# Left one-hots of a graph kernel's count matrix, groups innermost, code numbers read from SBUF

## What is computed

```
def step(h, _):
    messages = h[col] @ W_msg.T + b_msg
    agg = segment_sum(messages, row, num_segments=num_nodes)
    gi = agg @ W_ih.T + b_ih
    gh = h @ W_hh.T + b_hh
    r = sigmoid(i_r + h_r);  z = sigmoid(i_z + h_z)
    n = tanh(i_n + r * h_n)
    return ((1.0 - z) * n + z * h, None)
h, _ = lax.scan(step, relu(layernorm(x)), None, length=5)
return x + h
```

## Time and profile before

| | us |
|---|---|
| median of 3 runs | 5297.94 (5295.67 to 5298.79) |
| span of the profiled execution | 5295.2 |
| VectorE's first L1368 to its last L1374 | 219.5 to 834.3 |
| GpSimd's first L674 to its last | 117.2 to 960.9 |
| TensorE's first product on gathered rows | 976.5 |

### The profile page before, as it was taken

How to read it: one execution, slowest core, us unless ns; L and a number is a source line. 1 busy time by engine, 2 the same in 40 slices (tenths; PEclk the granted TensorE clock), 3 DMA queues, 4 the chain that set the end, 5 groups by cost and what they waited for, 6 DMA issues and landing times. The chain is left out here.

```text
span 5295.2 us, 80372 instructions
## 1 busy us (share of the span) xinstructions
PE 4969.6 (94%) x26501; PEld 2539.4 (48%) x26502; DVE 2590.3 (49%) x6993; ACT 861.8 (16%) x1421; POOL 3751.4 (71%) x3869
## 2 busy tenths in 40 slices
PE   5588888699999699999999999999999999999998
PEld 1344444355555345555555555555555555555554
DVE  8899993356666633433333433333343333333332
ACT  7666662000000000000000000000000000000000
POOL 3777777777776777677777677777767777757774
PEclk7799999899999799999999999999999999999999
DMA  5255555466666466666676666666666667566654
GB/s 170 68 165 164 164 165 167 118 183 183 175 174 173 114 195 182 185 181 181 176 203 179 183 180 181 180 188 192 178 184 181 181 179 212 177 182 188 189 177 125
DMA packets 1036729, 916.12 MB, mean 173 GB/s; under 512 B 507905, under 2 KB 771453, under 8 KB 1036412
## 3 DMA queue, kind: packets, MB, share of 16 engines
q1 hardware_dynamic: 482262, 661.95, 40.1%
q0 software_dynamic: 123920, 212.72, 15.0%
q10 hardware_dynamic: 430358, 39.09, 6.0%
HBM read 766.27 MB, written 147.15 MB: 172 GB/s over the span
## 5 line engine op out<-in xcount | busy, mean ns | idle before, releaser
L696 POOL DMA_INDIRECT f_ring<-fast_hrows,f_work x3175 | 3070.9, 967 | 1208.7 <-issue 950.6
L990 PE MATMUL f_ps_a<-f_ring,f_hr 128*128 128x512 fp8e4 (+1 forms) x13560 | 3017.1, 375 | 6.9 <-DMA f_ring<-fast_adj 6.9
L990 PEld LDWEIGHTS f_ps_a<-f_ring,f_hr 128*128 128x128 f16 x13560 | 1308.2, 98 | 1473.8 <-issue 138.2
L1500 DVE TENSOR_SCALAR f_ring<-f_iota_h,f_work 128x128 f16<-128x128 f16 (+1 forms) x3175 | 614.0, 283 | 1026.8 <-PE f_ps_a L1002 984.8
L674 POOL DMA_INDIRECT fast_rec<-f_slots x656 | 645.1, 983 | 213.7 <-issue 199.6
L1002 PE MATMUL f_ps_a<-f_ring 128*128 128x128 f16 (+1 forms) x5726 | 542.7, 237 | 62.9 <-DMA f_ring<-fast_hrows,f_work 62.7
L1424 DVE SCALAR_TENSOR_TENSOR f_work<-f_deg,f_bias_c,f_ps_c 128x512 f32<-128x512 f32 x125 | 93.5, 748 | 1009.8 <-PE f_ps_deg L1029 1009.8
L1002 PEld LDWEIGHTS f_ps_a<-f_ring 128*128 128x128 f16 x5726 | 440.8, 98 | 260.8 <-DMA f_ring<-fast_hrows,f_work 68.1
L792 ACT ACTIVATE f_work<-f_work,f_bsum 128x512 f32<-128x512 f32 x125 | 90.2, 722 | 2223.4 <-DVE f_work L1424 2223.4
L1374 DVE TENSOR_SCALAR f_ring<-f_iota_h,f_work 128x256 f16<-128x256 f16 x1536 | 413.2, 373 | 0.0
L949 PE MATMUL f_ps_deg<-f_ring,f_sel 128*128 128x512 fp8e4 x1536 | 395.6, 381 | 0.0
(11 more groups left out here) (322 smaller groups left out, 3164.3 us busy)
## 6 DMA issues: line engine op xcount, KB each, us to landing
f_ring<-fast_adj SPq DMA_DIRECT2D x750, 640.0 KB, 4.2
fast_adj<-f_ring SPq DMA_DIRECT2D x192, 512.0 KB, 3.2
f_ring<-fast_hrows,f_work POOLq DMA_INDIRECT x3175
f_deg<-fast_deg SPq DMA_DIRECT2D x125, 256.0 KB
fast_hrows<-f_work ACTq DMA_DIRECT2D x400, 64.0 KB
f_hr<-fast_hrows SPq DMA_DIRECT2D x24, 640.0 KB, 7.1
fast_rec<-f_slots POOLq DMA_INDIRECT x656, 2.4
fast_hrows<-f_deg SPq DMA_DIRECT2D x1, 6528.0 KB, 39.4
```

What stands on the lines that cost most here:

```text
L696: nc.gpsimd.indirect_dma_start(G[:, g * 2 * H:(g + 1) * 2 * H], None, hrows, bass.IndirectOffsetOnAxis(ap=idx_tab[:, col + g:col + g + 1], ...
L990: mm = pe.matmul(sumT[buf][:, 0:cols], lhsT=hr[:, t, a * H:(a + 1) * H], rhs=a_f8[:, t * CHUNK:t * CHUNK + cols], start=(t == 0 and a == 0 ...
L1500: ins = nc.vector.tensor_scalar(OH[:, g * HALF:g * HALF + w], iota_h[:, 0:w], loc[:, bass.ds(col + g, 1)], HOT, ALU.is_equal, ALU.mult)
```

## The change

The left one-hots of a batch are laid out with the eight groups innermost (element `c * 8 + g` in place of `g * 128 + c`). The code numbers are no longer in PSUM: one copy (128 x 1024) writes them eight times each into SBUF, into the space of `d2d`, whose contents are no longer needed. The comparison then reads both inputs from SBUF with eight float16 side by side. Before, its second input repeated one element 128 times. The products read their left one-hot with a step of eight elements (16 bytes). The number and order of instructions is as before on every engine.

```diff
-        iota_p = ps_m[:, 0:CHUNK // 2].bitcast(F16)
...
+        hot_l_of = [hot_l[:, a * BATCH * P:(a + 1) * BATCH * P].rearrange("p (c g) -> p c g", g=BATCH) for a in range(3)]
...
+        codes_iota = d2d[:, 0:BATCH * P // 2].bitcast(F16).rearrange("p (c g) -> p c g", g=BATCH)
...
-                        mm = pe.matmul(pairs[n % 3][:, a * HALF:(a + 1) * HALF], lhsT=hot_l[:, m * P:(m + 1) * P],
+                        mm = pe.matmul(pairs[n % 3][:, a * HALF:(a + 1) * HALF], lhsT=hot_l_of[slot][:, :, 4 * j + a],
...
-            link(nc.vector.tensor_copy(ps_m[:, 0:CHUNK // 2], iota_h[:].bitcast(F32)))
+            link(nc.vector.tensor_copy(codes_iota, iota_h[:, 0:P].unsqueeze(2).to_broadcast([P, P, BATCH])))
...
-                    nc.vector.tensor_tensor(
-                        hot_l[:, slot * BATCH * P:(slot + 1) * BATCH * P].rearrange("p (g c) -> p g c", c=P),
-                        iota_p[:, 0:P].unsqueeze(1).to_broadcast([P, BATCH, P]),
-                        codeT[:, bass.ds(col, BATCH)].unsqueeze(2).to_broadcast([P, BATCH, P]), ALU.is_equal)
+                    nc.vector.tensor_tensor(hot_l_of[slot], codes_iota,
+                                            codeT[:, bass.ds(col, BATCH)].unsqueeze(1).to_broadcast([P, P, BATCH]), ALU.is_equal)
```

More of the change, by code:

```diff
@@ L203, in build_fast @@
         assert at + 4 * K2 + K2 // 2 <= 8704 and 3 * GK * P <= at
+        assert 3 * GK * P <= at and BATCH * P // 2 <= K2
+        codes_iota = d2d[:, 0:BATCH * P // 2].bitcast(F16).rearrange("p (c g) -> p c g", g=BATCH)
         S_sb = work[:, 0:512].bitcast(F32)
```

## The result

The changed kernel takes 5313.43 us (5312.05 to 5316.28, 6 runs), the kernel before 5297.16 us beside it: a ratio of 1.0031, with a 95% interval of 1.0019 to 1.0042. It is 16 us slower, 0.3%, which is small but outside the spread of the runs. The prediction was 5319 us, slower, with a range of 5295 to 5385.

What follows compares the result with a forecast made beforehand. The prediction took the chain scatter, records, gather, TensorE as the bound, with the build beside it. Profiled span 5295.2 us + 21 for a later scatter end = 5316; runs stand 2.7 above, so 5319 us, range 5295 to 5385.

Runs made afterwards that it cites:

- the old comparison: The kernel before with only the comparison's code numbers read from SBUF in place of PSUM, layout and weights as before: 5419.1 us, ratio 1.0226.
- the short batch: The changed kernel with seven right one-hots to a batch of eight and three degree products of four: 5330 us (one run).

## What to carry to other kernels

Before an engine is made faster, look for the chain that ends behind its stage, and for whatever on that chain shares something with the instruction that is changed: here GpSimd's scatters, which lose time when they start within a comparison that reads two operands from SBUF, and a little at some of the right one-hots made from SBUF. Where one of two periodic streams can hold the other, the loss follows not from the length of the holding instruction but from the difference between the two rhythms, so a shorter instruction, or a shorter loop, can cost more. And when a rule says that something is slowed, look at the largest values and at a few rows in sequence, not at a median.

## What the runs showed that was not expected

- A packed comparison of 128 x 1024 float16 takes about the same time whether its numbers come from PSUM or from SBUF: 0.68 to 0.70 and 0.67 us.
- 128 x 256 float16 with two per-partition scalars takes 0.26 us from SBUF, start to start, and 0.32 us from PSUM.
- A scatter held by VectorE needs some 0.85 us from the end of the instruction that holds it: 0.85 behind L1352 and the old comparison, 0.84 behind the new one in the short batch and behind the first right one-hot (499.98 + 0.35 to 500.11 + 1.06). So it seems that 0.12 us of its 0.97 lie ahead of the point at which it waits.
- No version tried is clearly faster than the kernel before. While the scatter lasts to 957 us, at most 4 to 5 us are to be had from holds in the build, which is what taking away all of them gave (5293.3, inside its interval). The 76 scatters ahead of the build are busy 79.4 us, some 6 more than at 0.97 us each; no run tried those. The gap of 164 us on TensorE ahead of the gathered rows is open to whoever shortens the scatter: with 128 fewer in both, the changed kernel is 92 us faster than the one before.
